# A fused convolution and attention kernel: a second order of the calls on five engines and of four PSUM banks

## The chip, the cores and the metric

The kernel runs on one core of one Trainium2 chip. A core has five engines that run side by side, each working through its own list of instructions in order: PE (TensorE, matrix products), DVE (VectorE), ACT (ScalarE), POOL (GpSimd) and SP (SyncE, which here only issues DMA transfers). They wait for each other through semaphores. The metric is the time of one launch on the device, in microseconds.

## What is computed

The input x is 16 images of 32 x 32 pixels with 128 channels, in float32. Cut to what matters:

```
# first block, on h = x
perceived = depthwise 3x3 conv, 3 filters per channel (128 -> 384) + b_perc
hid   = gelu(w_up1 @ perceived + b_up1)            # 384 -> 256, exact gelu
h_new = h + w_up2 @ hid + b_up2                    # 256 -> 128
q, k, v = split(h_new @ w_qkv.T + b_qkv)
h1 = h_new + softmax over the 3x3 window(q . k / sqrt(128)) applied to v
# second block
xn = group_norm(h1, 8 groups, eps 1e-3) * gamma + beta
q, k, v = xn @ Wq + bq, xn @ Wk + bk, xn @ Wv + bv
out = xn + (softmax(q k^T / sqrt(128)) v) @ Wp + bp   # 1024 x 1024 scores per image
```

## The kernel before

One image is a chain of some hundred short calls on five engines. The 3x3 convolution and the first product are one Winograd convolution with six products in the rows' direction: `differences`, `transform`, `transform_even`, `transform_two` and `transform_ends` make its input, `conv(n, 0..5)` its products, and DVE's `sum_and_difference`, `combine`, `combine_own` and `end_row` put the products together in the tile u (L1851 to L1873). Then come `gelu`, `up2`, the projections `q`, `k`, `v`, the local attention (`local_scores`, `local_exp`, `local_probs_t`, `local_values`), `y_half`, the group norm (`channel_moments`, `group_moments`, `group_variance`, `inverse_deviation`, `group_norm`), and the second block: `qq`, `kk`, `vv`, eight score tiles per image (`scores`, `row_max`, `exp`), a turn of each tile of exponentials (`turn_e`, then through DRAM by SP's `send` and `fetch`, then `et_hi_tile` and `et_lo_tile`), four products `values(n, 0..3)`, `a_part`, `attended` and `output`.

Full precision comes from pairs: a tensor is split in a high part, made by ACT (`..._hi`), and a low part, made by DVE or POOL (`..._lo`), and each product is three matmuls (`mm3`, L576 to L578). PE's other matmuls are plain float32.

The order of the calls is written out by hand for each engine, in three programs: `fill_program`, `turn_program` and `drain_program`. A turn works on several images at once: in turn `it`, a = it is in its second attention, b = it + 1 in its local attention and group norm, c = it + 2 in its convolution and projections, d = it + 3 in its input transform, and z = it - 1 is being finished. Turns 1 to 12 run, the first written out, the others as a loop:

```python
            fill_program()
            turn_program(1)
            with eng.Fori(2, B - 3) as it:
                turn_program(it)
            drain_program()
```

Two score tiles (ps_s, ps_t) fill half of PSUM; the other half is four banks (`work`), which all other products use in turn. `BANK_PLAN`, `FILL_PLAN` and `DRAIN_PLAN` list each use with its bank, in PE's order; `previous_user` finds who had the bank last, and the new user waits until that one's result has been read (`bank_free`, `FREED_BY`). So the order of PE's calls and the choice of banks decide which reader on DVE or ACT PE waits for:

```python
        FREED_BY = dict(conv=u_step, up2=h_ready, q=q_ready, k=k_ready, v=v_ready,
                        at=pt_ready, av=y_ready, gn=gn_step, qq=qq_lo_ready, kk=kk_lo_ready,
                        vv=vv_lo_ready, pv=a_ready, pj=o_ready)
```

In these names `as` is `local_scores`, `at` is `local_probs_t`, `av` is `local_values`, `gn` is `group_moments`, `pv` is `values` and `pj` is `attended`. Before, in a turn, `values(a, 0)` takes the bank of `conv(c, 4)`, `v(c, 1)` that of `attended(a, 0)`, and `up2(c, 0)` that of `local_values(b, 0)`.

Of the kernel before, what the change touches and what calls it, by code (L numbers as in the profile page):

```python
# [57 lines left out]
class Count:  # L58
# [2318 lines left out]
```

How the kernel before makes its waits and increments, by code:

```python
            def store(n, k):  # L426
                sp.wait_ge(*o_ready.after(n, k))
                sp.dma_start(out_view[:, bass.ds(n * TILES + 4 * k, 4), :], r_tok[:, :, :]).then_inc(stored.handle, 16)
# [1 line left out]
            def send(n, t):  # L430
                sp.wait_ge(*e_turned.after(n, t))
                sp.dma_start(spread[t % 4].rearrange("p i c -> p (i c)"),
                             turned_both[:, t % 2].rearrange("p i k q -> p (i k q)")).then_inc(e_sent[t % 2].handle, 16)
# [1 line left out]
            def fetch(n, t):  # L436
                landed, read = e_sent[t % 2].after(n, t // 2), pe["pv"].after(n, t // 2 - 2)
                if not isinstance(n, int):
                    landed, read = ((handle, sp.to_reg(value)) for handle, value in (landed, read))
                sp.wait_ge(*landed)
                if t % 2 == 0:
                    sp.wait_ge(*read)
                if is_first(n) and t == 0:
                    sp.wait_ge(*g_lo_ready.after(1, 3))
                    sp.wait_ge(*h_ready.after(1, 1))
                for i in range(4):
                    sp.dma_start(et_f[32 * i:32 * (i + 1), t % 4].rearrange("r s k q -> r s (k q)"),
                                 spread[t % 4, :, i].rearrange("(s r) c -> r s c", s=4)) \
                      .then_inc(e_fetched[t % 4].handle, 16)
# [1 line left out]
            def load_x(n):  # L452
                sp.wait_ge(*xp_ready.after(n - 1, 1))
                for k in range(4):
                    load_channels(n, k)
```

## Time and profile before

| | us |
|---|---|
| median of 3 runs | 1090.01 |
| lowest, highest | 1089.63, 1095.34 |
| profiled execution | 1094.47 |
| its span, first to last instruction | 1092.7 |
| PE busy (share of the span) | 959.8 (88%) |
| DVE | 924.5 (85%) |
| ACT | 727.5 (67%) |
| POOL | 716.3 (66%) |
| mean granted TensorE clock | 0.961 |

The span covers one execution. Busy shares are means over fill, loop and drain; the loop, which repeats, is read by one of its periods. In the views a time is in microseconds from the start of the span, a line number names the line of the kernel that issued the instruction, and a note in square brackets says how long the engine sat idle before it and who released it.

### The profile page before, as it was taken

Reading aid. Unit: us, or ns where it says so; the run is one execution under the profiler, and the core shown is the slowest. Engines: PE = TensorE matmul, PEld = TensorE weight load, DVE = VectorE, ACT = ScalarE, POOL = GpSimd, SP = SyncE. Lnnn points to the kernel's source line nnn. Section 1 sums busy time; section 2 is a strip of 40 time slices with the busy share of each in tenths; the row PEclk is TensorE's granted clock in tenths of the full one; section 3 lists DMA queues with packets and bytes.
Section 4 is the critical chain, followed back from the end, with each engine's and each line's share of the span. In section 5 each row is a group of like instructions: output and inputs, shape, how many; then the busy total and the mean of one; then the engine's idle time right before and its main releaser. Section 6 shows DMA issues by size and latency. Waiting matters only on the chain.

```text
span 1092.7 us, 20391 instructions
## 1 busy us (share of the span) xinstructions
PE 959.8 (88%) x6036; PEld 862.8 (79%) x6036; DVE 924.5 (85%) x1628; ACT 727.5 (67%) x1379; POOL 716.3 (66%) x493
## 2 busy tenths in 40 slices
PE   5979898998888999888898988899888898989885
PEld 4968788787787888778797787888778788878775
DVE  6768898888989888898988889888898988987771
ACT  3466876676757767676666767767676676777662
POOL 3644685867667676776767566676775867665665
PEclk9999999999999999999999999999999999999897
DMA  5103465653655546355653655556355554545774
GB/s 89 21 1 85 134 159 169 155 150 101 173 161 123 153 151 169 103 142 168 141 163 115 147 159 126 144 158 169 96 153 164 134 163 132 149 144 154 209 232 138
DMA packets 177654, 152.88 MB, mean 140 GB/s; under 512 B 77776, under 2 KB 161104, under 8 KB 177616
## 3 DMA queue, kind: packets, MB, share of 16 engines
q1 hardware_dynamic: 176768, 152.03, 51.3%
q10 hardware_dynamic: 848, 0.39, 0.2%
q8 instruction: 19, 0.31, 0.1%
q14 instruction: 19, 0.16, 0.0%
HBM read 76.87 MB, written 75.50 MB: 139 GB/s over the span
## 4 chain that ended last, share of the span: by engine, by line
PE 45%; issue 15%; DVE 15%; POOL 4%; DMA 3%; SPq 2%; ACT 1%; DVEq 0%; ACTq 0%; POOLq 0%
PE work L576 9%; PE work L578 9%; PE work L577 9%; DVE turned L1997 3%; PE work L635 2%; DMA spread<-turned 2%; SPq L448 2%; PE ps_s L576 2%; PE work L669 2%; DVE nm L1990 2%; POOL et_lo L1508 2%; DVE gn L1959 2%; PE ps_t L576 2%; PE ps_t L577 2%; PE ps_t L578 2%
## 5 line engine op out<-in xcount | busy, mean ns | idle before, releaser
L1508 POOL TENSOR_TENSOR et_lo<-et_f,et_hi 128x1024 fp32r<-128x1024 f32 x128 | 319.2, 2501 | 129.5 <-ACT et_hi L1121 129.4
L1121 ACT ACTIVATE et_hi<-et_f 128x1024 fp32r<-128x1024 f32 x128 | 135.0, 1057 | 130.5 <-DMA et_f<-spread 130.5
L576 PE MATMUL work<-et_lo,vv_hi 128*128 128x256 f32 x512 | 158.4, 309 | 41.0 <-DVE u L1873 32.9
L576 PE MATMUL work<-t_lo,wc_hi 128*128 128x256 f32 x576 | 166.8, 290 | 0.0
L578 PE MATMUL work<-t_hi,wc_hi 128*128 128x256 f32 x576 | 162.6, 282 | 0.0
L577 PE MATMUL work<-t_hi,wc_lo 128*128 128x256 f32 x576 | 162.3, 282 | 0.0
L1997 DVE STREAM_TRANSPOSE turned<-e 128x1024 f32<-128x1024 f32 x128 | 154.0, 1227 | 9.7 <-ACT e L1116 6.8
L577 PE MATMUL work<-et_hi,vv_lo 128*128 128x256 f32 x512 | 155.4, 303 | 0.0
L578 PE MATMUL work<-et_hi,vv_hi 128*128 128x256 f32 x512 | 154.5, 302 | 0.0
L576 PEld LDWEIGHTS work<-et_lo,vv_hi 128*128 128x128 f32 x512 | 106.0, 207 | 44.4 <-DVE u L1873 31.6
L1508 POOL TENSOR_TENSOR g_lo<-u,g_hi 128x512 fp32r<-128x512 f32 x60 | 76.3, 1293 | 84.3 <-ACT g_hi L1034 84.3
L1508 POOL TENSOR_TENSOR t_lo<-t_f,t_hi 128x512 fp32r<-128x512 f32 x48 | 63.6, 1326 | 73.6 <-ACT t_hi L1008 73.2
L576 PEld LDWEIGHTS work<-t_lo,wc_hi 128*128 128x128 f32 x576 | 109.5, 190 | 2.0
L577 PEld LDWEIGHTS work<-t_hi,wc_lo 128*128 128x128 f32 x576 | 109.8, 191 | 0.7
L578 PEld LDWEIGHTS work<-t_hi,wc_hi 128*128 128x128 f32 x576 | 109.1, 189 | 0.0
L578 PEld LDWEIGHTS work<-et_hi,vv_hi 128*128 128x128 f32 x512 | 107.4, 210 | 0.0
L577 PEld LDWEIGHTS work<-et_hi,vv_lo 128*128 128x128 f32 x512 | 106.1, 207 | 0.6
L1990 DVE TENSOR_REDUCE nm<-ps_t 128x1 f32<-128x1024 f32 x64 | 77.8, 1216 | 10.0 <-PE ps_t L578 10.0
L1116 ACT ACTIVATE e<-ps_s,nm 128x1024 f32<-128x1024 f32 x64 | 71.2, 1112 | 20.5 <-DVE nm L1990 19.9
L576 PE MATMUL ps_s<-kk_lo,qq_hi 128*128 128x512 f32 x128 | 55.5, 433 | 28.3 <-ACT e L1116 28.3
L1990 DVE TENSOR_REDUCE nm<-ps_s 128x1 f32<-128x1024 f32 x64 | 77.7, 1214 | 2.6 <-PE ps_s L578 2.2
L1116 ACT ACTIVATE e<-ps_t,nm 128x1024 f32<-128x1024 f32 x64 | 70.9, 1108 | 3.5 <-DVE nm L1990 3.4
(181 smaller groups left out, 2680.7 us busy)
## 6 DMA issues: line engine op xcount, KB each, us to landing
spread<-turned SPq DMA_DIRECT2D x128, 512.0 KB, 3.0
et_f<-spread SPq DMA_DIRECT2D x512, 128.0 KB, 3.5
x_in<-in_x SPq DMA_DIRECT2D x64, 128.0 KB, 4.2
out<-r_tok SPq DMA_DIRECT2D x32, 256.0 KB, 3.7
w_up_t<-in_L_conv_w_up SPq DMA_DIRECT2D x1, 384.0 KB, 4.1
y<-in_L_conv_w_qkv SPq DMA_DIRECT2D x1, 192.0 KB, 4.7
const<-in_const ACTq DMA_DIRECT2D x1, 166.0 KB, 5.1
y<-in_L_conv_w_up ACTq DMA_DIRECT2D x1, 128.0 KB, 4.9
```

What stands on the lines that cost most here:

```text
L448: sp.dma_start(et_f[32 * i:32 * (i + 1), t % 4].rearrange("r s k q -> r s (k q)"), spread[t % 4, :, i].rearrange("(s r) c -> r s c", s=4)) \
L576: te.matmul(dst, wh, xl, start=first, stop=False)
L577: te.matmul(dst, wl, xh, start=False, stop=False)
L578: return te.matmul(dst, wh, xh, start=False, stop=last)
L635: mm = te.matmul(bank("v", half, n)[:, t * 128:(t + 1) * 128], h[:, pix], wv0[:, :], start=True, stop=True)
L669: te.matmul(dst[:, u * 128 - before:(u + 1) * 128 + behind], v_pix[:, t, :], pt[half][:, at - before:at + 128 + behind], start=(u == 0), s ...
L1116: act.activation(e_both[:, t % 2], score_tile(n, t)[:, :], ACT.Exp, bias=nm1[:, t:t + 1], accum_out=sum1[:, t:t + 1]) \
L1121: act.activation(et_hi[:, t % 4].rearrange("p s k q -> p (s k q)"), et_f[:, t % 4].rearrange("p s k q -> p (s k q)"), ACT.Copy).then_inc(e ...
L1508: return pool.tensor_tensor(dst, full, hi, ALU.subtract)
L1959: dve.tensor_tensor(gn_a, gamma, rstd, ALU.mult).then_inc(gn_step.handle, 1)
L1990: dve.tensor_reduce(nm1[:, t:t + 1], score_tile(n, t)[:, :], AX.X, ALU.max, negate=True) \
L1997: dve.transpose(turned_both[:, t % 2].rearrange("p i k q -> p k i q"), e_both[:, t % 2].rearrange("p (k i q) -> p k i q", k=TILES, i=4)).t ...
```

## The change

Every call keeps its operations and buffers. What changes is the order of the calls in the three programs of each engine, and with it the three bank plans. The cut between two turns lies elsewhere: `values(a, 3)`, `attended(a, 1)`, `local_scores(c, 3)`, `local_probs_t(c, 1)` and the first two convolutions of image d now end a turn, where they began the next one. Of the new loop plan, `values(a, 0)` takes the bank of `conv(c, 5)`, `up2(c, 0)` that of `values(a, 0)`, `vv(a, 1)` that of `conv(c, 0)`, `kk(b, 0)` that of `attended(a, 0)`, and `v(c, 1)` that of `k(c, 0)`. The core of the diff, in the turn's programs (fill and drain are changed in the same manner):

```diff
 BANK_PLAN = [
-    ("conv", 5, 2, 3), ("av", 0, 1, 0), ("pv", 0, 0, 1), ("av", 1, 1, 3), ("up2", 0, 2, 0), ("gn", 0, 1, 3),
...
@@ PE, turn_program
                 vv(a, 1)
-                values(z, 3)
                 scores(a, 4)
-                attended(z, 1)
-                conv(c, 0)
-                local_probs_t(b, 1)
-                local_scores(b, 3)
                 scores(a, 5)
-                conv(c, 1)
                 conv(c, 2)
...
+                q(c, 0)
+                values(a, 1)
                 k(c, 0)
-                values(a, 1)
-                q(c, 0)
                 attended(a, 0)
                 values(a, 2)
-                v(c, 1)
+                kk(b, 0)
                 qq(b, 0)
                 qq(b, 1)
-                kk(b, 0)
+                v(c, 1)
                 kk(b, 1)
...
                 local_probs_t(c, 0)
+                values(a, 3)
+                local_scores(c, 3)
+                conv(d, 0)
+                attended(a, 1)
+                conv(d, 1)
+                local_probs_t(c, 1)
@@ ACT, turn_program
+                et_hi_tile(a, 3)
+                a_part(a, 0)
                 gelu(c, 2)
                 gelu(c, 3)
                 g_hi_part(c, 2)
                 g_hi_part(c, 3)
-                a_part(a, 0)
                 h_hi_half(c, 0)
...
+                exp(b, 3)
+                take(d, 0, 1)
+                et_hi_tile(b, 0)
@@ DVE, turn_program
                 y_half(b, 0)
                 y_half(b, 1)
+                channel_moments(b)
                 h_half(c, 0)
-                channel_moments(b)
...
                 turn_e(a, 6)
                 turn_e(a, 7)
+                group_norm(b)
                 output(a, 0)
@@ drain, PE
                 scores(B - 1, 2)
                 scores(B - 1, 3)
-                values(B - 2, 3)
-                attended(B - 2, 1)
+                values(B - 2, 2)
                 scores(B - 1, 4)
                 scores(B - 1, 5)
+                values(B - 2, 3)
+                vv(B - 1, 1)
+                attended(B - 2, 1)
```

Three places show what moves. The first is DVE in the loop, around the work on u (`sum_and_difference` is L1851 and L1852, or L1863 and L1864 in the changed file, `combine` the two instructions after them). Before:

```order
L1851 TENSOR_TENSOR u<-u,work 128x16x32
L1852 TENSOR_TENSOR u<-u,work 128x16x32
L1924 STREAM_TRANSPOSE pt<-pn 32x2x32
L1925 STREAM_TRANSPOSE pt<-pn 32x2x32
L1851 TENSOR_TENSOR u<-u,work 128x16x32
L1852 TENSOR_TENSOR u<-u,work 128x16x32
L1858 SCALAR_TENSOR_TENSOR u<-u 128x16x32 x2
L1865 SCALAR_TENSOR_TENSOR u<-u 128x16x32 x2
L1873 TENSOR_TENSOR u<-u,work 128x16x32 x2
```

and the changed kernel, from `output(z, 1)` on (its reciprocal is the row ahead of r_tok):

```order
L2021 SCALAR_TENSOR_TENSOR r_tok<-work,rec,r_tok 128x128 x4
L1927 RECIPROCAL rec<-sum 128x2 x2
L1995 TENSOR_TENSOR vv_lo<-work,vv_hi 128x512
L2002 TENSOR_REDUCE nm<-ps_s 128x1
L2002 TENSOR_REDUCE nm<-ps_t 128x1
L1936 STREAM_TRANSPOSE pt<-pn 32x2x32
L1937 STREAM_TRANSPOSE pt<-pn 32x2x32
L2009 STREAM_TRANSPOSE turned<-e 128x8x4x32
L1863 TENSOR_TENSOR u<-u,work 128x16x32
L1864 TENSOR_TENSOR u<-u,work 128x16x32
L1870 SCALAR_TENSOR_TENSOR u<-u 128x16x32 x2
L1877 SCALAR_TENSOR_TENSOR u<-u 128x16x32 x2
```

The two sums and differences stood close together; now `output`, two row maxima and a transpose of exponentials stand between the first and the second.

The second place is SP's queue in the loop, in the first turn (spread<-turned is `send`, et_f<-spread `fetch` of one tile by four transfers, out<-r_tok `store`, x_in<-in_x `load_x`). Before, from `store(z, 0)` on:

```order
L428 DMA out<-r_tok 128x4x128
L413 DMA x_in<-in_x 32x32x32 x4
L433 DMA spread<-turned 128x1024 x3
L448 DMA et_f<-spread 32x4x256 x8
L428 DMA out<-r_tok 128x4x128
L448 DMA et_f<-spread 32x4x256 x4
```

and in the changed kernel, again from `store(z, 0)` on:

```order
L433 DMA spread<-turned 128x1024 x2
L448 DMA et_f<-spread 32x4x256 x8
L428 DMA out<-r_tok 128x4x128
L433 DMA spread<-turned 128x1024
L448 DMA et_f<-spread 32x4x256 x4
L433 DMA spread<-turned 128x1024
L413 DMA x_in<-in_x 32x32x32 x4
L448 DMA et_f<-spread 32x4x256 x4
```

The third tile's `send` stood ahead of the second store; now it stands behind it, and the input loads stand between the fourth tile's `send` and its `fetch`.

The third place is DVE between the projections of the second attention and its first row maximum (`kk_lo` and `qq_lo`, then the input transform: t_f by L1753 or L1765 is `transform_two`, by L1762 `transform_ends`, d<-xp is `transform_even`; max_mark opens `local_mask_max`). Before:

```order
L1743 SCALAR_TENSOR_TENSOR d_54<-xp 128x256
L1744 SCALAR_TENSOR_TENSOR d_54<-xp 128x256
L1887 SCALAR_TENSOR_TENSOR qq_lo<-work,cols,qq_hi 128x512 x2
L1887 SCALAR_TENSOR_TENSOR kk_lo<-work,cols,kk_hi 128x512 x2
L1753 SCALAR_TENSOR_TENSOR t_f<-d_53 128x8x32 x2
L1762 SCALAR_TENSOR_TENSOR t_f<-d_53 128x8x32 x2
L1905 MEMSET max_mark 128x1
```

and in the changed kernel:

```order
L1899 SCALAR_TENSOR_TENSOR kk_lo<-work,cols,kk_hi 128x512
L1899 SCALAR_TENSOR_TENSOR qq_lo<-work,cols,qq_hi 128x512 x2
L1904 TENSOR_TENSOR v_pix<-work,bv_row 128x512
L1899 SCALAR_TENSOR_TENSOR kk_lo<-work,cols,kk_hi 128x512
L1765 SCALAR_TENSOR_TENSOR t_f<-d_53 128x8x32 x2
L1755 SCALAR_TENSOR_TENSOR d_54<-xp 128x256
L1756 SCALAR_TENSOR_TENSOR d_54<-xp 128x256
L1917 MEMSET max_mark 128x1
```

`transform_ends` has left this place (it now follows the second transpose of the next image's exponentials), and `transform_even` and a part of `v_half` have come in.

## Rows read from the trace of the kernel before

**Rows 1.** The page's first line.
```profile
span 1092.7 us, 20391 instructions
```
**Rows 2.** Stages: length, PE, PEld, DVE, ACT, POOL busy, clock, DMA share, GB/s.
```profile
782.60:847.40 64.80, 58.04 (x375) 52.56 (x375) 57.73 (x101) 44.91 (x85) 44.17 (x31) 0.97 0.53 145
...
808.90:812.00 3.10, 3.09 (x14) 2.50 (x15) 2.88 (x13) 2.85 (x8) 0.39 (x1) 1.00 0.26 107
...
838.00:842.00 4.00, 4.00 (x24) 4.00 (x24) 3.89 (x7) 3.76 (x8) 1.73 (x2) 0.64 0.15 59
```
**Rows 3.** Waits of PE in 782.6 to 847.4: total us, times, longest.
```profile
PE work L576 <- DVE u L1873: 2.9, 1, 2.9
PE ps_s L576 <- ACT e L1116: 2.1, 1, 2.1
PE work L680 <- DVE moments L1943: 1.5, 2, 0.8
PE work L635 <- DVE r_tok L2009: 1.0, 1, 1.0
```
**Rows 4.** Timeline of PE: start, length, instruction; L680 is group_moments, L635 v.
```profile
195.92 0.38 PE L680 MATMUL work<-moments,const 128*128 128x2 f32 x2 [0.77 <-DVE moments L1943]
...
782.53 0.38 PE L680 MATMUL work<-moments,const 128*128 128x2 f32 x2 [0.75 <-DVE moments L1943]
...
795.94 0.46 PE L635 MATMUL work<-wv,h 128*128 128x128 f32 x2 [1.05 <-DVE r_tok L2009]
...
912.22 0.38 PE L680 MATMUL work<-moments,const 128*128 128x2 f32 x2 [0.77 <-DVE moments L1943]
```
**Rows 5.** Timeline of DVE in a loop period.
```profile
788.77 2.23 DVE L1959 TENSOR_TENSOR gn<-cols,gn 128x1 f32<-128x1 f32 x1
...
792.21 2.37 DVE L1997 STREAM_TRANSPOSE turned<-e 128x1024 f32<-128x1024 f32 x2
...
802.54 3.31 DVE L1762 SCALAR_TENSOR_TENSOR t_f<-d 128x256 f32<-128x256 f32 x2
...
830.19 5.71 DVE L1858 SCALAR_TENSOR_TENSOR u<-u 128x512 f32<-128x512 f32 x2
```
**Rows 6.** Timeline of POOL in the same period.
```profile
788.59 2.39 POOL L1508 TENSOR_TENSOR et_lo<-et_f,et_hi 128x1024 fp32r<-128x1024 f32 x1
792.58 2.54 POOL L1508 TENSOR_TENSOR xn_lo<-y,xn_hi 128x512 fp32r<-128x512 f32 x2 [1.60 <-ACT xn_hi L1090]
...
830.18 5.17 POOL L1508 TENSOR_TENSOR et_lo<-et_f,et_hi 128x1024 fp32r<-128x1024 f32 x2 [0.30 <-ACT et_hi L1121]
```
**Rows 7.** Timeline of DVE in the fill, the same instructions.
```profile
26.79 1.11 DVE L1762 SCALAR_TENSOR_TENSOR t_f<-d 128x256 f32<-128x256 f32 x2
...
39.38 1.28 DVE L1858 SCALAR_TENSOR_TENSOR u<-u 128x512 f32<-128x512 f32 x2
```
**Rows 8.** Timeline of SP, which issues the transfers.
```profile
800.82 3.09 SPq L413 DMA_DIRECT2D x_in<-in_x  x4
...
840.61 0.81 SPq L433 DMA_DIRECT2D spread<-turned  x2
844.61 3.65 SPq L448 DMA_DIRECT2D et_f<-spread  x8
```
**Rows 9.** Timeline of ACT: the first tile sent at 840.61.
```profile
849.13 1.06 ACT L1121 ACTIVATE et_hi<-et_f 128x1024 fp32r<-128x1024 f32 x1 [1.86 <-DMA et_f<-spread]
```
**Rows 10.** The page's DMA issues: count, KB each, median us from issue to landing.
```profile
out<-r_tok SPq DMA_DIRECT2D x32, 256.0 KB, 3.7
```
**Rows 11.** DVE's groups by line in 782.6 to 847.4: busy us, mean ns, idle before.
```profile
L1997 DVE STREAM_TRANSPOSE turned<-e 128x1024 f32<-128x1024 f32 x8 | 9.6, 1224 | 0.3 <-ACT e L1116 0.3
L1990 DVE TENSOR_REDUCE nm<-ps_s 128x1 f32<-128x1024 f32 x5 | 6.1, 1212 | 0.0
...
L1983 DVE TENSOR_TENSOR vv_lo<-work,vv_hi 128x512 fp32r<-128x512 f32 x2 | 1.3, 672 | 0.7 <-ACT vv_hi L1108 0.7
```
**Rows 12.** Timeline of PE in the drain.
```profile
982.00 0.47 PE L576 MATMUL work<-g_lo,w_hi 128*128 128x512 f32 x1 [2.01 <-DVE h L1880]
```

More of the change, by code:

```diff
@@ L820, in fill_program @@
                 scores(0, 5)
+                local_values(1, 0)
+                local_probs_t(1, 2)
                 scores(0, 6)
-                local_probs_t(1, 2)
-                local_values(1, 0)
                 local_probs_t(1, 3)
                 up2(2, 0)
-                vv(0, 1)
+                scores(0, 7)
                 local_values(1, 1)
+                values(0, 0)
+                group_moments(1)
+                up2(2, 1)
                 v(2, 0)
-                values(0, 0)
+                q(2, 0)
                 k(2, 0)
-                scores(0, 7)
-                up2(2, 1)
-                group_moments(1)
-                q(2, 0)
+                v(2, 1)
                 values(0, 1)
-                q(2, 1)
-                k(2, 1)
-                attended(0, 0)
-                kk(1, 0)
-                kk(1, 1)
-                qq(1, 0)
-                qq(1, 1)
-                v(2, 1)
-                local_scores(2, 0)
+                k(2, 1)
+                kk(1, 0)
+                qq(1, 0)
+                kk(1, 1)
+                attended(0, 0)
+                local_scores(2, 0)
+                q(2, 1)
                 scores(1, 0)
@@ L1631, in fill_program @@
                 xn_lo_half(1, 1)
-                differences(3)
+                transform(3)
                 et_lo_tile(0, 4)
@@ L1703, in drain_program @@
                 xn_lo_half(B - 1, 1)
+                residual(B - 2, 0)
                 et_lo_tile(B - 2, 4)
@@ L2093, in fill_program @@
                 local_mask_max(1, 0)
[L2094 to L2095 removed]
                 turn_e(0, 0)
                 turn_e(0, 1)
+                local_rec(1, 0)
                 row_max(0, 2)
[L2099 removed]
+                local_mask_max(1, 1)
                 row_max(0, 3)
+                transform_two(2)
                 turn_e(0, 2)
+                local_mask_max(1, 2)
                 halo_turn(1, 0)
+                local_rec(1, 1)
+                transform_ends(2)
+                turn_e(0, 3)
+                row_max(0, 4)
                 sum_and_difference(2, 1, 2, 1)
[L2104 to L2105 removed]
                 sum_and_difference(2, 3, 0, 3)
[L2107 removed]
                 local_mask_max(1, 3)
@@ L2121, in fill_program @@
                 halo_turn(1, 2)
-                turn_e(0, 4)
+                vv_lo_half(0, 1)
                 halo_turn(1, 3)
@@ L2125, in fill_program @@
                 h_half(2, 0)
-                vv_lo_half(0, 1)
+                turn_e(0, 5)
+                row_max(0, 6)
                 y_half(1, 1)
-                row_max(0, 6)
                 channel_moments(1)
-                v_half(2, 0)
-                turn_e(0, 5)
                 turn_e(0, 6)
                 row_max(0, 7)
+                h_half(2, 1)
+                v_half(2, 0)
                 group_variance(1)
-                h_half(2, 1)
                 group_norm(1)
@@ L2139, in fill_program @@
                 turn_e(0, 7)
-                output(0, 0)
+                v_half(2, 1)
+                transform_even(3)
                 kk_lo_half(1, 0)
@@ L2211, in turn_program @@
                 transform_two(d)
-                transform_ends(d)
+                transform_even(d)
                 local_mask_max(c, 0)
                 row_max(b, 0)
+                row_max(b, 1)
                 local_rec(c, 0)
-                row_max(b, 1)
                 turn_e(b, 0)
                 local_mask_max(c, 1)
+                turn_e(b, 1)
+                transform_ends(d)
+                local_rec(c, 1)
                 local_mask_max(c, 2)
                 halo_turn(c, 0)
-            def drain_program():
-                local_rec(B - 2, 1)
-                row_max(B - 3, 2)
-                row_max(B - 3, 3)
-                turn_e(B - 3, 1)
-                turn_e(B - 3, 2)
-                vv_lo_half(B - 3, 0)
+                row_max(b, 2)
@@ L2232, in drain_program @@
+                local_mask_max(c, 3)
+                vv_lo_half(b, 0)
+                row_max(b, 3)
+                halo_turn(c, 1)
+                turn_e(b, 2)
+            def drain_program():
                 output(B - 4, 1)
+                local_rec(B - 2, 2)
+                turn_e(B - 3, 3)
+                sum_and_difference(B - 1, 1, 2, 1)
                 row_max(B - 3, 4)
-                local_mask_max(B - 2, 3)
-                row_max(B - 3, 5)
                 vv_lo_half(B - 3, 1)
-                turn_e(B - 3, 3)
@@ L2251, in drain_program @@
                 end_row(B - 1, 5, 3, 7)
-                row_max(B - 3, 6)
                 halo_turn(B - 2, 3)
+                row_max(B - 3, 5)
+                turn_e(B - 3, 4)
                 y_half(B - 2, 0)
@@ L2256, in drain_program @@
                 channel_moments(B - 2)
+                row_max(B - 3, 6)
+                group_variance(B - 2)
+                group_norm(B - 2)
+                turn_e(B - 3, 5)
                 turn_e(B - 3, 6)
-                group_variance(B - 2)
+                h_half(B - 1, 0)
                 row_max(B - 3, 7)
-                group_norm(B - 2)
-                h_half(B - 1, 0)
                 h_half(B - 1, 1)
-                qq_lo_half(B - 2, 0)
                 kk_lo_half(B - 2, 0)
-                turn_e(B - 3, 7)
                 kk_lo_half(B - 2, 1)
                 output(B - 3, 0)
+                qq_lo_half(B - 2, 0)
+                turn_e(B - 3, 7)
                 qq_lo_half(B - 2, 1)
@@ L2302, in drain_program @@
                 row_max(B - 2, 7)
+                turn_e(B - 2, 5)
                 group_variance(B - 1)
@@ L2319, in drain_program @@
                 turn_e(B - 1, 3)
-                output(B - 2, 1)
                 row_max(B - 1, 4)
                 row_max(B - 1, 5)
+                output(B - 2, 1)
+                turn_e(B - 1, 4)
                 vv_lo_half(B - 1, 0)
                 vv_lo_half(B - 1, 1)
-                turn_e(B - 1, 4)
                 turn_e(B - 1, 5)
```

605 lines of the change are left out of this document (291 added, 314 removed), and 53 rows, old and new, of tables (BANK_PLAN, DRAIN_PLAN, FILL_PLAN).

## Prediction

> **What bounds the kernel now.** I read the views from coarse to fine. The page gives a span of 1092.7 us [rows 1]; the time of that execution is 1094.47. Most of the span is the loop: PE's `group_moments`, run once per image, started at 195.92 in the first turn and at 912.22 in the twelfth [rows 4], so eleven periods took 716.3 us, 65.1 each. The table by stage for one quiet period, 782.6 to 847.4, shows that no engine is full: PE 58.0 and DVE 57.7 busy of 64.8, ACT 44.9, POOL 44.2, DMA 53% [rows 2]. So the question is which waits the period is made of. The view of waits for PE in that window names four: 2.9 us at `values(a,0)` for DVE's u, 2.1 at `scores(b,2)` for an exponential, 1.0 at `v(c,1)` for `output`, and 0.8 (the larger of two) at `group_moments` [rows 3]. Together 6.8. A fifth cost hides in the busy time: from 838 to 842, right after the 2.9 us wait, the granted clock was 0.64 (a mix of 1.2 and 2.4 GHz), against 1.00 in 808.9 to 812, right after the 2.1 us wait [rows 2]. That is 4.0 x 0.36 = 1.4 us. So 8.2 of 64.8 are lost, and some 56.6 are PE's work.
>
> Why is u late? DVE's two `combine` calls (L1858) took 5.71 us together, from 830.19 [rows 5]; in the fill the same two took 1.28 [rows 7]. POOL's two `et_lo` ran from 830.18 to 835.35 [rows 6]. In the same way `transform_ends` (L1762 x2) took 3.31 at 802.54 against 1.11 in the fill [rows 5, 7], and L1959 took 2.23 and ended at 791.00 when POOL's `et_lo`, begun at 788.59, ended at 790.98 [rows 5, 6]. A DVE instruction that reads two SBUF operands stands still until the POOL instruction in progress ends.
>
> **The change, part by part (per period).** Operations and buffers are the same. Turns are cut at another place: two convolutions, `values(.,3)`, two et tiles and a residual go into the turn before. By itself that is a relabelling and costs nothing in the loop; what counts is the order across the cut.
>
> *u chain.* At the moment DVE starts `combine`, which POOL work is in progress? Now `output(z,1)` stands just ahead, and SP sends e tile 2 only after storing that output. A tile sent at 840.61 was in `et_hi` at 849.13 [rows 8, 9], 8.5 us; then comes `et_hi`, 1.06 [rows 9]. So `et_lo(a,2)` can begin some 10 us after `output`. DVE's work between `output` and `combine` is two row maxima and one transpose (1.21, 1.21, 1.22), one vv_lo at 0.67 [rows 11], and small calls that I put at 2.2 (an estimate: a sum and difference like two vv_lo, 1.3, and 0.9 for reciprocals and halo): 6.5. Its four instructions of u at 0.65 each (the fill's 1.28 for two [rows 7]) are over at 9.1, before POOL's tile. POOL's residual, freed by the store (3.7 to land [rows 10], 4.1 with its issue), runs from 4.1 to 6.7 and touches the first by 0.2. So the 2.9 us wait and its 1.4 of clock go: -4.3. Bounds: -4.3, and nothing if one `et_lo` (2.6, half of 5.17 [rows 6]) comes first and something else fills the rest. I take -4.3, since the distance is some 1 us.
>
> *scores.* `transform_ends` (3.31 [rows 5]) leaves the place ahead of `row_max(b,0)`, and the shorter `transform_even` moves in about the same place. The 2.1 us wait for that tile's exponential [rows 3] goes but for 0.2: -1.9. Bounds -2.1 and 0. Late next is `transform_ends` itself; its reader, `conv(d,4)`, is a turn's start away.
>
> *moments.* `channel_moments` moves ahead of `h_half(c,0)`; -0.8 [rows 3], bounds -0.8 and 0.
>
> *normalization.* `turn_e(a,6)` and `(a,7)`, 2.37 [rows 5], now precede `group_norm`, and `kk(b,0)`, which needs xn_lo, precedes `v(c,1)`, so the 1.0 wait at v is replaced by one at kk. Before, the first xn_lo ended at 792.58 + 1.27 = 793.9 [rows 6], 11.3 after `group_moments` at 782.53 [rows 4]; PE reached v at 795.94 - 1.05 = 794.9, 12.4 after it [rows 4]. 11.3 + 2.37 = 13.7: a wait of 1.3. Bounds: 0 if L1959 no longer meets a POOL instruction (2.2 saved), 2.5 if DVE also stands 1.2 for an exponential. Net +0.3.
>
> *vv(a,1)* takes the bank that `conv(c,0)` filled, read by `take(c,0)`, now last but one in ACT's turn; I put 0.4 on it (an estimate, by laying ACT's calls against PE's), bounds 0 and 2.1, the nearest wait for ACT [rows 3].
>
> *up2(c,0)* takes the bank of `values(a,0)`, freed by `a_part(a,0)`, which ACT does only after `et_hi(a,3)`. That tile's turn_e ends; sum and difference (1.3), four instructions of u (2.6) and two end rows (1.3) follow on DVE, then PE runs `values` (24 x 0.12 = 2.9) and `av` (1.4): PE asks 9.6 after it. The tile needs the 8.5 of [rows 8, 9], more because the four x loads (3.09 to issue [rows 8]) and fetch(a,2) stand ahead on SP: I take +1.6; then 1.06 and 0.4 for `et_hi` and `a_part`: 11.6. A new wait of 2.0. Bounds 0 and 6 (both delays in full, 3.1 and one fetch, 1.8).
>
> Sum: -4.3 - 1.9 - 0.8 + 0.3 + 0.4 + 2.0 = -4.3. Three meetings of DVE and POOL (L1762 after `transform`, L1943 after `et_lo(a,3)`, L1959) are decided by tenths; half of one costs 0.3. So -4.0 a period, 61 us. Eleven periods: -44.
>
> *Drain and fill.* The drain's first image repeats the turn; its wait of 2.01 [rows 12] and the like give -3. At the end scores 4 and 5 of the last image now precede `values(B-2,3)`, some 3 us of PE, so the final chain starts earlier: -3. The fill is bound by weights and by PE; 0, bounds -4 and +4. Total -50: 1094.5 would become 1044.5. The median of the runs shown, 1090.01, lies 4.5 below the profiled execution, so I write **1042**.
>
> **A rule against the sum.** Here the 2.1 us wait cost no clock and the 2.9 us wait did [rows 2, 3]; my longest new wait is 2.0, so the sum has no clock loss. The Trainium skill, in "TensorE: Matmul & The Clock Gate", section "What's actually happening", says that the throttled state is the default and that only activity lifts it. By that rule two waits close together could each bring half speed; that is the third rival.
>
> **Rivals.** (1) *The lock stays on the u chain*: if `output` is late or a transfer early, `et_lo(a,2)` starts before `combine`. Against it: the 1 us of distance. Price: 2.7 us of the removed wait return, or -1.3 a period: 1094 - 14 - 3 = 1077. (2) *Slower: the e tiles' round trips in series.* Tile 2 waits for the store, tile 3 for tile 2's fetch and the x loads, and PE waits at `up2` for `et_hi(a,3)`. For it: ACT already sits idle 1.9 for a tile [rows 9]. Break-even is a wait of 4.9, since -8.2 + 1.9 (the other new waits) + 4.9 + 1.4 (clock) = 0, that is, `et_hi(a,3)` beginning over 13 us after its transpose instead of 8.5. At 6.0: +1.1 a period, 1094 + 12 - 3 = 1103, 1100 beside the median. (3) *Half speed after the new waits*: twice 1.4, or -1.2 a period: 1078. (4) *Nothing gained*: PE's next want shows up after each removed wait: 1090.
>
> **Chances.** Forecast 0.60; rivals (1) 0.14, (2) 0.11, (3) 0.08, (4) 0.07. Within 0.5% is about what a measurement of this kernel can't tell from no change. Faster: 0.60 + 0.14 + 0.08 = 0.82; same 0.07; slower 0.11. The range's low end takes both large new waits at half or less, -6.6 a period and -6 outside: 1016. The high end takes in rivals (1) and (3): 1083. That leaves out (2) and (4), 0.18.
>
> **What would show it.** Right: the period from `group_moments` to `group_moments` near 61; no PE wait for u; L1858 near 0.65 each; a PE wait of 1 to 3 us at `up2` after a_part, another at `kk` for xn_lo; granted clock near 1.0 through `values(a,0)`. Wrong: L1858 still at 2.8; a wait at `up2` above 4.9; or a period at 64 with waits of other names.

## The result, and the profile after

The changed kernel takes 1010.04 us (median of 4 runs, 1007.96 to 1010.71), beside 1089.83 for the kernel before in the same comparison: a ratio of 0.9253, 95% interval 0.9221 to 0.9285. The gain is 79.8 us; 50 was forecast, and the time lies below the low end of the range, 1016. The profiled execution took 1010.17, its span is 1008.4, 84.3 less than in [rows 1].

The stage table of the changed kernel, cut at `group_moments` of images 0, 1, 2, 13 and 14, and then one stretch of 4 us (columns as in [rows 2]):

```profile
82.75:131.66 48.91, 44.73 (x280) 39.39 (x281) 41.95 (x87) 38.91 (x74) 25.80 (x22) 1.00 0.42 119
131.66:190.35 58.69, 55.04 (x370) 49.96 (x369) 51.56 (x99) 43.44 (x87) 44.97 (x31) 1.00 0.61 171
190.35:838.07 647.72, 618.86 (x4116) 564.27 (x4115) 552.41 (x1100) 498.62 (x937) 471.66 (x331) 0.99 0.60 161
838.07:894.38 56.31, 54.70 (x370) 49.75 (x369) 48.80 (x99) 44.28 (x82) 42.98 (x30) 1.00 0.48 140
894.38:1008.40 114.02, 94.31 (x544) 82.29 (x542) 72.29 (x136) 66.63 (x122) 71.51 (x40) 0.90 0.67 194
542.00:546.00 4.00, 4.00 (x25) 3.44 (x23) 3.25 (x7) 2.86 (x5) 3.74 (x4) 1.00 0.99 238
```

The same stages before:

```profile
82.36:136.01 53.65, 49.66 (x295) 43.51 (x296) 46.42 (x90) 39.09 (x76) 29.65 (x24) 0.97 0.42 109
136.01:195.92 59.91, 54.31 (x352) 48.89 (x351) 54.64 (x99) 41.79 (x82) 43.98 (x30) 0.97 0.61 167
195.92:912.22 716.30, 640.89 (x4115) 579.51 (x4115) 636.99 (x1101) 493.94 (x935) 489.47 (x331) 0.97 0.54 145
912.22:975.35 63.13, 58.02 (x375) 52.51 (x375) 56.46 (x101) 45.36 (x83) 43.34 (x29) 0.97 0.46 135
975.35:1092.70 117.35, 94.33 (x538) 82.85 (x536) 74.06 (x134) 68.43 (x122) 71.08 (x40) 0.89 0.63 184
```

The third line of each is the loop: eleven periods in 647.72 instead of 716.30, so 58.9 each instead of 65.1. That is -68.6; the fill gives -5.6 up to image 2's `group_moments` (195.92 against 190.35), the drain's first image -6.8, and the rest to the end -3.3. PE's time in the loop splits in two: idle 75.4 before and 28.9 after, and busy 22.0 less for the same matmuls.

Where the idle time was and is, by the waits of PE over the whole loop, before:

```profile
PE work L576 <- DVE u L1873: 30.4, 11, 3.2
PE ps_s L576 <- ACT e L1116: 22.9, 11, 2.1
PE work L635 <- DVE r_tok L2009: 12.2, 11, 1.3
PE work L680 <- DVE moments L1943: 9.2, 12, 0.8
```

and after, which is the whole list:

```profile
PE work L579 <- ACT a_c L1133: 19.2, 11, 2.3
PE work L579 <- POOL xn_lo L1517: 7.1, 9, 0.9
PE work L707 <- ACT a_c L1133: 2.6, 9, 0.4
```

None of the four old waits is left. The two that the prediction put in their place, `up2` for `a_part` and `kk` for xn_lo, are there; a third, at `attended`, is small. Why the old ones went is in the timelines of DVE and POOL in the period that starts at 486.54, where [rows 5, 6] had 5.71, 3.31 and 2.23:

```profile
530.75 1.29 DVE L1870 SCALAR_TENSOR_TENSOR u<-u 128x512 f32<-128x512 f32 x2
531.96 1.28 DVE L1877 SCALAR_TENSOR_TENSOR u<-u 128x512 f32<-128x512 f32 x2
...
553.55 0.90 DVE L1971 TENSOR_TENSOR gn<-cols,gn 128x1 f32<-128x1 f32 x1
...
571.22 1.09 DVE L1774 SCALAR_TENSOR_TENSOR t_f<-d 128x256 f32<-128x256 f32 x2
```

```profile
521.92 4.76 POOL L1517 TENSOR_TENSOR et_lo<-et_f,et_hi 128x1024 fp32r<-128x1024 f32 x2 [2.27 <-ACT et_hi L1127]
526.68 1.29 POOL L1576 TENSOR_TENSOR r_tok<-vv_hi,vv_lo 128x512 f32<-128x512 f32 x1
528.05 1.29 POOL L1579 TENSOR_TENSOR r_tok<-r_tok,bp_row 128x512 f32<-128x512 f32 x1
533.45 2.38 POOL L1517 TENSOR_TENSOR et_lo<-et_f,et_hi 128x1024 fp32r<-128x1024 f32 x1 [4.10 <-ACT et_hi L1127]
```

POOL's residual is over at 529.34, 1.4 us before `combine` begins at 530.75. The next et tile begins at 533.45, only 0.2 us after `combine_own` (L1877), which ends at 533.24. Over the eleven periods that last distance is 0.14 to 0.44, and the two pairs take 1.28 or 1.29 in each of them.

### The profile page after: what moved, and what is told of

The parts are those of the page before. It is cut to its first block, busy times and chain, and to the rows that moved or that the text cites. A ratio compares the mean times of both kernels' runs of the same rounds, so it can differ in the third digit from the quotient of the medians.

```text
span 1008.4 us, 20393 instructions
## 1 busy us (share of the span) xinstructions
PE 930.4 (92%) x6036; PEld 841.8 (83%) x6036; DVE 821.2 (81%) x1628; ACT 733.4 (73%) x1381; POOL 694.5 (69%) x493
## 4 chain that ended last, share of the span: by engine, by line
POOL 36%; issue 31%; PE 19%; ACT 4%; DMA 4%; DVE 3%; SPq 1%; POOLq 1%; ACTq 0%; DVEq 0%
POOL et_lo L1517 18%; POOL g_lo L1517 4%; PE work L579 4%; PE work L581 4%; PE work L580 4%; POOL d L1523 3%; POOL r_tok L1576 3%; POOL t_lo L1517 3%; POOL xn_lo L1517 2%; DMA et_f<-spread 2%; POOL h_lo L1517 2%; DMA spread<-turned 1%; SPq L448 1%; DVE turned L2009 1%; PE work L651 1%
## 5 line engine op out<-in xcount | busy, mean ns | idle before, releaser
L1517 POOL TENSOR_TENSOR et_lo<-et_f,et_hi 128x1024 fp32r<-128x1024 f32 x128 | 305.3, 2401 | 161.6 <-ACT et_hi L1127 161.6
L2009 DVE STREAM_TRANSPOSE turned<-e 128x1024 f32<-128x1024 f32 x128 | 157.1, 1237 | 31.8 <-ACT e L1122 29.0
L579 PE MATMUL work<-et_lo,vv_hi 128*128 128x256 f32 x512 | 151.0, 295 | 8.3 <-POOL et_lo L1517 6.2
L580 PE MATMUL work<-et_hi,vv_lo 128*128 128x256 f32 x512 | 148.0, 289 | 0.0
L581 PE MATMUL work<-et_hi,vv_hi 128*128 128x256 f32 x512 | 147.1, 287 | 0.0
L579 PEld LDWEIGHTS work<-et_lo,vv_hi 128*128 128x128 f32 x512 | 99.2, 194 | 10.1 <-POOL et_lo L1517 6.9
L580 PEld LDWEIGHTS work<-et_hi,vv_lo 128*128 128x128 f32 x512 | 99.0, 193 | 0.9
L581 PEld LDWEIGHTS work<-et_hi,vv_hi 128*128 128x128 f32 x512 | 99.4, 194 | 0.0
L1070 ACT ACTIVATE p<-p,nm 128x204 f32<-128x204 f32 x128 | 57.9, 459 | 3.0 <-DVE nm L1920 1.4
```

The costliest lines, as they stand in the source:

```text
L579: te.matmul(dst, wh, xl, start=first, stop=False)
L580: te.matmul(dst, wl, xh, start=False, stop=False)
L581: return te.matmul(dst, wh, xh, start=False, stop=last)
L1070: ins_ = act.activation(tile, tile, ACT.Exp, bias=nm0[:, t:t + 1], scale=-1.0, accum_out=sum0[:, t:t + 1])
L1517: return pool.tensor_tensor(dst, full, hi, ALU.subtract)
L2009: dve.transpose(turned_both[:, t % 2].rearrange("p i k q -> p k i q"), e_both[:, t % 2].rearrange("p (k i q) -> p k i q", k=TILES, i=4)).t ...
```

## The experiments

The edits are in the program of the loop's turn, unless said otherwise. "Period" is the loop's length, cut as above, over eleven.

### Does POOL alone make u late?

`spare_work` subtracts a row from itself twice, 128 x 896, into a tile that nobody reads.

```diff
@@ after: POOL, turn_program
                 residual(b, 0)
+                spare_work()
```

> The changed kernel (1010.0 us) with two extra POOL instructions per loop turn, placed behind residual(b,0): each subtracts a broadcast row from itself into a spare tile that nobody reads (some 2.1 us each, an estimate from et_lo's 2.4 for 1024 columns against 896 here). They would run from about 529.3 to 533.5 of the period that starts at 486.5, over DVE's combine, which begins at 530.75, and are over when et_lo(a,2) begins at 533.45. Nothing depends on them. Theory (a DVE instruction with two SBUF operands stands still while a POOL instruction runs, and this alone made u late in the kernel before): L1870 and its neighbour take about 4 us together instead of 1.29, so u comes 2.7 later; u now has some 0.4 to spare, so PE waits about 2.3 for u per period, with up to 1.4 of clock behind it, from which the present wait of 1.6 at up2 may give back some. Net +1 to +3.5 per period, 1022 to 1050 us. Rival (the pair was slow before for another reason, for instance its neighbours on DVE or the banks it reads): L1870 stays at 1.29, no wait for u, time within 3 us of 1010.

Measured: 1039.5 us (ratio to before 0.9514, 0.9474 to 0.9553), period 61.3. Line numbers are 7 higher in this kernel: L1877 is `combine`, L1884 `combine_own`. DVE and POOL at the place:

```profile
481.54 2.89 DVE L1877 SCALAR_TENSOR_TENSOR u<-u 128x512 f32<-128x512 f32 x2
484.35 3.44 DVE L1884 SCALAR_TENSOR_TENSOR u<-u 128x512 f32<-128x512 f32 x2
```

```profile
480.11 3.77 POOL L1572 TENSOR_TENSOR spare<-bp_row 128x896 f32<-128x896 f32 x2
484.23 2.41 POOL L1518 TENSOR_TENSOR et_lo<-et_f,et_hi 128x1024 fp32r<-128x1024 f32 x1 [0.35 <-ACT et_hi L1128]
```

Nothing waits for the spare tile, and still the two pairs take 6.3 us instead of 2.6; the second pair has slipped under the et tile that the order had just missed. PE waits 34.1 us for u in eleven periods, and over the 4 us after one such wait of 3.11 the granted clock is 0.60 (behind two of the eleven it stays at 1.00). The theory holds. In the changed kernel `combine` clears the next POOL instruction by 1.4 us, and the last of u's locked instructions by 0.2.

### transform_ends back in its old place

```diff
@@ after: DVE, turn_program
                 local_mask_max(c, 0)
+                transform_ends(d)
                 row_max(b, 0)
...
                 turn_e(b, 1)
-                transform_ends(d)
```

> The changed kernel with one call put back: transform_ends(d) stands again ahead of row_max(b,0) in DVE's turn. The prediction's scores term says that this place cost 1.9 us per period; undoing it alone would then give +1.9 x 11 = +21, 1031 us, with a wait for an exponential at scores(b,2) on PE and a long L1774 (over 2 us for the pair) beside a POOL instruction. Rival: since the other waits on DVE are gone, DVE now runs ahead of PE there, and 1.1 us more ahead of row_max(b,0) is within its slack: 1010 to 1015 us, no wait at scores(b,2).

Measured: 1088.9 us (0.9966, 0.9938 to 0.9993), period 65.5. Undoing the move of this one call, 1.09 us for its pair, takes back nearly the whole gain. DVE, POOL and PE:

```profile
671.01 5.39 DVE L1774 SCALAR_TENSOR_TENSOR t_f<-d 128x256 f32<-128x256 f32 x2
```

```profile
670.97 4.95 POOL L1517 TENSOR_TENSOR et_lo<-et_f,et_hi 128x1024 fp32r<-128x1024 f32 x2 [3.59 <-ACT et_hi L1127]
```

```profile
678.86 0.59 PE L579 MATMUL ps_s<-kk_lo,qq_hi 128*128 128x512 f32 x1 [4.73 <-ACT e L1122]
```

In [rows 5] the pair met one et tile and took 3.31. In the new order POOL does tiles 6 and 7 one right behind the other, and each of the two instructions stands for one of them. From 678 to 682, behind the wait of 4.73, the granted clock is 0.64. So the place costs 6.6 per period in the new order; neither the term (1.9) nor the rival foresaw that. If each POOL instruction over the pair costs its own length, moving tile 7 away must bring back about a third:

```diff
@@ on top of it: POOL, turn_program
-                et_lo_tile(a, 7)
                 transform(d)
+                et_lo_tile(a, 7)
```

> The run with transform_ends(d) put back (1088.9 us, period 65.5 instead of 58.9) with one POOL call moved as well: et_lo_tile(a,7) goes behind transform(d), so that one et tile and not two lies over the pair L1774. Theory (each POOL instruction over the pair costs its own length, which is why the old place cost 6.6 per period in the new order and only 0.9 to 1.9 in the old one): the pair takes 3.0 to 3.5 us instead of 5.39, the wait for an exponential at scores(b,2) falls from 4.7 to 2.2 to 2.6, -2.2 to -3.5 per period with the clock behind it: 1050 to 1065 us. Rival (transform_ends costs its place there whatever POOL does, for instance through the late row maxima alone): within 8 us of 1089, the pair still above 4.5.

Measured: 1070.8 us (0.9813, 0.9763 to 0.9863), period 63.6, pair 3.77, wait at the scores 3.12. The forecast was missed in size: the pair was to take 3.0 to 3.5, the wait 2.2 to 2.6 and the whole 1050 to 1065. The gain of 1.9 per period is under the forecast 2.2 to 3.5, because `transform`'s own first instruction (0.99 us from 659.43), which now follows the tile, stands over the second of the pair; that reason is read from the timeline and not tried. In kind the theory holds: the rival had the pair above 4.5 and the time within 8 us of 1089.

### One part alone, in the kernel before

```diff
@@ before: DVE, turn_program
-                transform_ends(d)
                 local_mask_max(c, 0)
...
                 turn_e(b, 0)
+                transform_ends(d)
```

> The kernel before (1089.8 us) with one part of the change alone: transform_ends(d) goes behind turn_e(b,0) in DVE's turn. The scores term by itself: -1.9 x 11 = -21, 1069 us, the wait at scores(b,2) (22.9 us in eleven periods) gone or under 5. Rival 1: the wait for u, which comes later in the period, grows by what is gained, since u is bound by POOL's tiles and not by PE: 1085 to 1090. Rival 2: transform_ends meets another POOL instruction in its new place and holds up the turns of e: the wait at scores(b,2) moves to another reader, 1080 or more.

Measured: 1082.6 us beside 1091.9 for the kernel before in the same comparison (0.9909, 0.9875 to 0.9943). The 22.9 us of waits at the scores fell to 1.0, but 0.9 per period of 2.1 came out: the wait for u stayed (28.4), and small waits for nm, qq_lo and pt came up.

```diff
@@ before: POOL, turn_program
-                et_lo_tile(a, 2)
                 g_lo_part(c, 0)
                 g_lo_part(c, 1)
+                et_lo_tile(a, 2)
```

> The kernel before (1089.8 us) with one POOL call moved in the turn: et_lo_tile(a,2) goes behind g_lo_part(c,1), so that one et tile and not two runs over DVE's combine. Theory (each POOL instruction over the pair costs its own length): L1858's pair takes 3.3 us instead of 5.71, u comes 2.4 earlier, the wait for u (30.4 us in eleven periods) falls to about 0.5 each and the clock behind it (0.64 over 838 to 842) stays at 1.0: -2.4 to -4.1 per period, 1045 to 1064 us. Rival (terms are not additive: moving transform_ends alone gave -0.9 per period where 1.9 was forecast, with small waits of other names in its place): about half, 1068 to 1080. Second rival: the et tile behind g_lo holds up g_lo(c,2) by 1.6 us and PE waits at up2(c,1): no gain, 1085 or more.

Measured: 1103.7 us, slower (1.0110, 1.0058 to 1.0162). The wait for u fell from 30.4 to 4.9 us as forecast, yet 23.8 appeared at `local_values(b,1)` for ACT's `pt_pair`, and v's wait for `output` rose from 12.2 to 19.3. Both parts together:

> The kernel before with both single moves: transform_ends(d) behind turn_e(b,0) on DVE, and et_lo_tile(a,2) behind g_lo_part(c,1) on POOL. If the two locks are independent terms, its gain is the sum of the two single gains (the first alone gave -9.4 us, the second is measured beside this run). If each hides part of the other, so that both must go before PE can use the time, the gain is larger than the sum by 5 us or more: the prediction's -1.9 and -4.3 x 0.85 per period would give -5.5 x 11 = -61, 1029 us. If the waits behind them take over (for v, for moments, for pn), the gain is smaller than the sum.

Measured: 1093.4 us (1.0002, 0.9973 to 1.0030). Nothing, though PE now waits only 4.8 us for u and 0.8 at the scores in the whole loop. The largest wait in their place is for `pt_pair`, 27.1 us in the loop. In one period it looks like this, with ACT's work ahead of it:

```profile
514.76 0.40 PE L669 MATMUL work<-pt,v_pix 128*128 128x160 f32 x1 [2.50 <-ACT pt L1082]
```

```profile
509.49 1.10 ACT L1116 ACTIVATE e<-ps_t,nm 128x1024 f32<-128x1024 f32 x1
510.49 0.19 ACT L1116 ACTIVATION_READ_ACCUMULATOR e<-ps_t,nm 128x1 f32 x1
510.69 1.28 ACT L1029 ACT_TABLE_LOAD   x1
511.99 1.33 ACT L1029 ACTIVATE u<-u,cols 128x512 f32<-128x512 f32 x2
513.23 1.13 ACT L1034 ACTIVATE g_hi<-u 128x512 fp32r<-128x512 f32 x2
514.27 0.36 ACT L1082 ACTIVATE pt<-work 128x256 f32<-128x256 f32 x1
```

`pt_pair(b,3)` (L1082, 0.36 us) stands behind a tile, an exponential, a table load and two gelu. While PE stood for u, this wait was hidden under it. (It is not the whole account: PE's idle time in the loop fell by 9.4 us, and its busy time rose by 9.3, from 640.9 to 650.2; the second was not traced.) The change moves `pt_pair`, which the prediction did not price. So three of its ACT moves were added:

```diff
@@ before, with both parts: ACT, turn_program
-                et_hi_tile(a, 3)
+                pt_pair(b, 3)
                 exp(a, 5)
                 gelu(c, 0)
-                gelu(c, 1)
                 g_hi_part(c, 0)
+                gelu(c, 1)
                 g_hi_part(c, 1)
-                pt_pair(b, 3)
+                et_hi_tile(a, 3)
```

> The kernel before with the two single moves of the run on both locks (1093.4 us) and three ACT moves that the change makes too: pt_pair(b,3) ahead of exp(a,5), et_hi_tile(a,3) behind g_hi_part(c,1), and g_hi_part(c,0) ahead of gelu(c,1). Theory: freeing u gave nothing because the next want, local_values(b,1), waits for pt_pair(b,3), which stood behind the two gelu on ACT (30.1 us in 13 turns), and up2 behind it would wait for g_lo; both hang on u through ACT. With ACT in the new order the wait of 2.5 for pt goes, g_lo of the first part is there some 2.5 us earlier, and the u term is paid out: -2 to -3.5 per period against the run on both locks, 1055 to 1071 us. Rival: yet another want follows (v for output, 1.8 each there, moments, g_lo): less than 1 per period, above 1082. The change's full gain of 6.2 per period is not expected in any case, since v's wait for output is untouched.

Measured: 1056.0 us (0.9678, 0.9642 to 0.9715), period 62.4, 37.4 less than without the ACT moves. With u's lock and ACT's order together the kernel gains, where the u part alone gained nothing. The three ACT moves were not run without the other two, so how much of the 37.4 they would give by themselves is not shown. The waits that are left are `v` for `output` (19.1 us) and moments (15.2).

### The other terms, undone or pushed further

Only the third and the last line lie wholly outside the changed kernel's own interval (0.9221 to 0.9285); for the others the profile says more than the time.

| one call moved in the changed kernel (1010.0) | us | ratio to before |
|---|---|---|
| DVE: `channel_moments(b)` behind `h_half(c,0)` again | 1009.3 | 0.9232 (0.9193 to 0.9270) |
| ACT: `a_part(a,0)` ahead of `et_hi_tile(a,3)` | 1007.5 | 0.9222 (0.9186 to 0.9257) |
| SP: `load_x(d)` behind `fetch(a,3)` | 1035.2 | 0.9472 (0.9436 to 0.9507) |
| DVE: `group_norm(b)` ahead of `turn_e(a,6)` | 1004.7 | 0.9209 (0.9184 to 0.9234) |
| ACT, drain: `exp(B-1,5)` ahead of `et_hi_tile(B-1,1)` | 1010.1 | 0.9258 (0.9232 to 0.9284) |
| ACT and DVE: the second and the fourth line together | 1001.1 | 0.9160 (0.9131 to 0.9190) |

```diff
@@ first line: DVE, turn_program
-                channel_moments(b)
                 h_half(c, 0)
+                channel_moments(b)
```

> The changed kernel with one call put back: channel_moments(b) stands again behind h_half(c,0) in DVE's turn. The prediction's moments term was 0.8 us per period, so +9, 1019 us, with a wait for moments at group_moments on PE. Theory of a larger term: h_half needs up2(c,0), which now starts only after its own 1.6 us wait, so moments (1.15 to 2.06 us) would start after about 543.3 of the period that starts at 486.5 and end near 545, where PE asks at 543.96: 1 to 2 us per period, 1021 to 1032 us. Rival: nothing is gained or lost, 1008 to 1013 us, because the wait at v or at kk takes it up.

Nothing lost: a wait for moments of 6.4 us came back in the loop, and xn_lo's halved (7.1 to 3.5). The moments term is worth nothing where the next want, `kk`, takes it up.

```diff
@@ second line: ACT, turn_program
+                a_part(a, 0)
                 et_hi_tile(a, 3)
-                a_part(a, 0)
```

> The changed kernel (1010.0 us) with one ACT call moved in the turn: a_part(a,0) goes ahead of et_hi_tile(a,3), so the bank that up2(c,0) waits for is free when values(a,0) has ended and not when tile 3 has come back from DRAM. Theory: the wait for a_c (19.2 us in eleven periods, 1.75 each) goes; g_lo ends some 0.4 after PE asks and moments some 0.6 after it would ask then, so 0.7 to 1.35 per period are left as gain: 995 to 1002 us. Rival: the wait only changes its name to g_lo or moments (or kk, which waits for xn_lo), 1007 to 1011 us.

The wait for a_c at `up2` is gone, and the loop's waits are now these five, 26.1 us instead of 28.9:

```profile
PE work L579 <- POOL xn_lo L1517: 8.2, 11, 0.8
PE work L579 <- POOL g_lo L1517: 6.3, 11, 0.7
PE work L707 <- ACT a_c L1133: 4.3, 11, 0.6
PE work L638 <- DVE h L1892: 4.1, 11, 0.4
PE work L683 <- DVE moments L1955: 3.2, 11, 0.5
```

The rival was right: the most visible wait was covered by others nearly its own size.

```diff
@@ third line: SP, turn_program
-                load_x(d)
                 fetch(a, 3)
+                load_x(d)
```

> The changed kernel with one call moved on SP's queue in the turn: the four x loads go behind fetch(a,3). They take 3.37 us to issue and stand between send(a,3) and fetch(a,3). Theory: et_hi(a,3) begins up to 2.5 us earlier, about 537.2 to 538 of the period that starts at 486.5 instead of 539.69, so the wait at up2 (1.75 per period) goes, and et_lo(a,3) with it begins earlier and leaves DVE's moments alone: -0.7 to -1.6 per period, 992 to 1002 us. Rival: the transfer of tile 3, not its place in the queue, sets its time, and the fetch now runs against the x loads on the DMA engines: 1007 to 1012 us, wait at up2 above 1.2.

Neither theory had it slower. The wait at `up2` did go, but the loads now stand between `fetch(a,3)` and `send(a,4)`, and the next pair of tiles is late: `attended(a,0)` waits for its `a_part` 33.8 us in eleven periods, up to 4.2, and the loop's clock falls to 0.97. The loads take some 3 us of the queue, and the tile behind them is late in either place; the place that the change chose is the cheaper of the two.

```diff
@@ fourth line: DVE, turn_program
+                group_norm(b)
                 turn_e(a, 6)
                 turn_e(a, 7)
-                group_norm(b)
```

> The changed kernel (1010.0 us) with group_norm(b) ahead of turn_e(a,6) and turn_e(a,7) in DVE's turn. Theory: the wait at kk(b,0) for xn_lo (7.1 us in nine of eleven periods, 0.8 each) exists because the two turns stand first; it goes, the tiles 6 and 7 come 0.9 later with room before values(a,3): -0.5 to -0.8 per period, 1001 to 1005 us. Rival: group_norm waits for POOL's inverse_deviation, and DVE stands still for it where it now turns tiles; the tiles 6 and 7, late by more than 1 us, hold up POOL's et_lo and transform: 1008 to 1016 us.

As the theory has it: -5.4 us by the medians, -4.8 by the ratios, and xn_lo's waits in the loop go from 7.1 to 0.3.

```diff
@@ fifth line: ACT, drain_program
                 vv_hi_half(B - 1, 0)
+                exp(B - 1, 5)
                 et_hi_tile(B - 1, 1)
-                exp(B - 1, 5)
```

> The changed kernel (1010.0 us) with one call moved in ACT's drain: exp(B-1,5) ahead of et_hi_tile(B-1,1). Its row maximum is there at 965.4, but ACT stands at et_hi for tile 1's transfer and does the exponential only at 970.96; PE waits 2.81 for it at scores(B-1,7). Theory: the exponential runs at about 968.2, scores(B-1,7) starts 2.7 earlier, and so do values(B-1,0), the fetch of tile 4 that waits for it, and the end: -1.5 to -2.7, 1007.3 to 1008.5 us. Rival: values(B-1,0) then waits for et_lo of tile 1 (over at 973.5) and the last transfers set the end: 1009 to 1011 us.

A miss: the exponential moved and the wait for it shrank from 2.81 to 1.0, and 2.18 appeared at `values(B-1,0)` for et_lo. The tail is bound by the tiles, as the rival says.

The last line is the second and the fourth edit in one kernel:

> The changed kernel (1010.0 us) with the two single moves that gained: a_part(a,0) ahead of et_hi_tile(a,3) on ACT (1007.5 alone) and group_norm(b) ahead of turn_e(a,6) and (a,7) on DVE (1004.7 alone). If the waits behind a_part are what kk's wait gave back (xn_lo 0.7 per period stood there in the run with a_part alone), the two together give more than their sum of 7.9: 1.75 + 0.65 less the waits for g_lo, moments and attended's a_part that appeared (about 1.3) is 1.1 per period, 998 us. If each only hands its time to the same third wait: 1003 to 1005. Additive: 1002.

It beats both kernels: period 58.2, 8.9 us below the changed kernel where the two single moves gave 7.9. They are nearly separate costs.

## Why the prediction was right in direction and short in size

- **u chain.** Right at the place: no wait for u in the loop, and its four instructions L1870 and L1877 over before the tile. The first experiment shows the cause. The distance of about 1 us that the prediction worked out, from the end of these four to the tile, came out at 0.2, with 2.2 us of the way put in by estimate; that the order misses the tile is in part luck.
- **clock.** Forecast 1.4 per period; 1.5 came by the rows below, and PE's busy time fell by 2.0.
- **scores.** The wait went entirely, 2.1 instead of 1.9. The reason was narrower than stated: not that a long call leaves the place, but that it leaves the et tiles, of which the new order puts two there.
- **moments and normalization.** The wait at `kk` was forecast at 1.3 and measured 7.1 us over eleven periods, 0.65 each. L1971 took 0.90 in the quoted period where L1959 took 2.23, so most of its bound "0 if L1959 no longer meets a POOL instruction" came true.
- **vv and the races.** Forecast 0.4 and 0.3, found nothing; an unforeseen 0.24 stood at `attended`.
- **up2.** Forecast 2.0, measured 19.2 / 11 = 1.75. The mechanism was right: with `a_part` ahead of the tile the wait is gone (second line of the table). The prediction's 9.6 adds up to 9.5, so its terms make 2.1.

The clock term was read behind one wait. Read in the same way (length times what the clock lacks of 1.00) over the 8 us behind each of the eleven waits for u, it is 1.4 to 1.7. But a wait at the scores, which the prediction had without a loss, had one of 1.7 in one of the eleven periods before, behind 2.07 us:

```profile
613.26:617.26 4.00, 4.00 (x11) 3.14 (x12) 3.76 (x14) 2.83 (x8) 0.38 (x1) 0.57 0.32 131
```

And in the changed kernel two of the eleven waits at `up2`, of 2.32 and 1.74, are followed by a loss:

```profile
246.76:250.76 4.00, 4.00 (x12) 3.15 (x13) 0.75 (x1) 2.84 (x5) 3.35 (x2) 0.63 0.74 185
250.76:254.76 4.00, 4.00 (x23) 3.45 (x22) 2.92 (x6) 2.33 (x3) 4.00 (x5) 0.94 0.44 85
482.21:486.21 4.00, 4.00 (x12) 3.14 (x13) 2.82 (x2) 2.85 (x5) 3.42 (x3) 0.64 0.82 203
```

By these rows the loss went from some 20 us in the loop to 3.4. The 0.5 per period by which PE's busy time fell beyond that was not traced.

The step that failed is the sum, "So -4.0 a period, 61 us. Eleven periods: -44.": its new waits (2.0, 1.3, 0.4, 0.2 and 0.3 for races, 4.2 together) each came out smaller than stated, and 2.63 came in all (28.9 / 11). PE's busy time fell by 2.0 where the clock term had 1.4. Together that makes 2.2 per period, 24 of the 34 us of difference in the spans. The second is "The fill is bound by weights and by PE; 0": it gave 5.6. The profile before shows that the fill too had a wait for u, and one for the local attention's pn, each with a lower clock behind it (0.79 over the 8 us from 121.95, 0.65 over the 4 us from 185.99):

```profile
121.95 0.44 PE L657 MATMUL work<-const,pn 128*128 128x128 f32 x2 [3.35 <-ACT pn L1073]
...
185.99 0.36 PE L576 MATMUL work<-et_lo,vv_hi 128*128 128x256 f32 x1 [2.56 <-DVE u L1873]
```

In the changed kernel these two are 1.6 and 1.5 long, and the clock is 1.00 over both of the fill's stages.

The third is the drain's first image, -6.8 instead of -3; the stretch has the waits of one more period (2.1, 1.9, 1.0 and 0.8 before, 1.6 in all after), and one of the loop's gave 6.2. The tail's -3 was right as a sum (-3.3). The low end took waits at half in the loop (-6.6 per period, against -6.2), but only -6 outside it, against -15.7. (By the medians the gain is 79.8 and not 84.3, since the profiled execution before lay 4.6 above its median. The prediction lowered its forecast for that, by 2.5 and not by the 4.5 that it names, and its low end not at all: 1094.5 - 72.6 - 6 is 1016, 1011 beside the median. The measured 1010 lies below that too.) What made the fill and drain gain was read from the profiles and not tried by itself.

Of the rivals, (1) had its mechanism right, and its price of 2.7 a period is near the 2.4 (61.3 - 58.9) of the first experiment; but the order misses the tile, by 0.2 us. (2) is real for single moves: the SP move shows some 3 us of the queue per period turning into 25 us over the launch. (3) came in two of the eleven periods and cost 3.4 us in all, where it was priced at twice 1.4 in each; in the others, as behind the wait of 1.63 (542 to 546), the clock is 1.00. The Trainium skill's page "TensorE: Matmul & The Clock Gate", section "What's actually happening", says that the throttled state is the default and that activity releases it. The rows agree with the release: behind the wait of 2.32 the clock is 0.63 and then 0.94, and 1.00 over the next 4 us. (4) was the deepest miss. It got 0.07 as a fate of the whole change, and it is the fate of most parts taken alone: u alone +12 us, u with scores +2, moments undone 0. The prediction treated the terms as independent. That it still came near is, as far as these runs show, because the change moves the next wants as well.

The Trainium skill's page "SBUF — State Buffer", section "SBUF: two separate sides", says that a DVE instruction with two SBUF inputs and a POOL instruction that reads SBUF share one port pair: whichever starts first has it for the whole instruction, and the other is blocked. The runs agree: 5.39 for a pair over two tiles of 2.4, 3.77 over one and a shorter one, 1.09 over none.

## What to carry to other kernels

A wait that is removed pays only as far as the next want of the same engine is early; look for what the wait has been hiding (here a 0.36 us copy behind two gelu) and move that too, or measure nothing. Where two engines block each other by whole instructions, list what the other has in progress at the start of each short call that the bounding engine waits for: a call of 1 us at the wrong place cost 79 us over eleven periods. And when several small costs are each rounded up, the sum is biased; carry the unshaded sum as the forecast and the shading in the range.

## What the runs showed of the hardware that was not expected

The length of a wait alone does not tell what clock follows it. In the run with the spare POOL work two waits for u at the same instruction, of 3.10 and 3.11 us, were followed by these 4 us:

```profile
367.63:371.63 4.00, 4.00 (x31) 4.00 (x32) 3.89 (x6) 3.85 (x7) 2.48 (x2) 1.00 0.48 178
489.04:493.04 4.00, 4.00 (x21) 4.00 (x22) 3.89 (x6) 3.52 (x5) 2.48 (x2) 0.61 0.44 169
```

The first kept 2.4 GHz, the second is a mix of 1.2 and 2.4. In the changed kernel a wait of 1.74 was followed by 0.64. Nor does the sum of the idle time tell it. In the kernel before with five moves PE stood idle for 51.6 of 686.3 us, in waits of at most 1.8, and the loop's granted clock was 1.00; in the run with the loads moved it stood idle for less, 43.1 of 672.1, in waits of up to 4.2, and the loop's clock was 0.97:

```profile
194.04:880.37 686.33, 634.76 (x4114) 562.16 (x4114) 610.92 (x1101) 492.62 (x935) 477.32 (x331) 1.00 0.56 151
```

```profile
190.86:862.96 672.10, 628.98 (x4115) 575.94 (x4114) 542.85 (x1100) 497.51 (x936) 471.59 (x331) 0.97 0.58 154
```

What decides it is not shown by these runs. A clock loss read behind one wait is therefore to be checked in the other periods before it goes into a sum.

And two DVE instructions in a row over two POOL instructions in a row do not wait for both and then run: POOL's two tiles take 4.95 instead of the 4.76 at 521.92 above, and DVE's pair ends 0.5 after them, so one of the pair ran between the tiles, at a cost to POOL of some 0.2.
